# Three MLP steps in token halves at the start of an attention and MLP kernel

## What is computed

```python
x = x + layernorm(attn(layernorm(x)))          # x: (8, 512, 128)
x = x + layernorm(ffn(layernorm(x)))

def attn(x):      # linear attention, 4 heads of 32
    xn = (x - mean) / sqrt(var + eps) * gamma + beta
    q, k, v = split(xn @ w_qkv)
    k = softmax(k, over the tokens)
    context = k.T @ v; out = (q * 32 ** -0.5) @ context   # by head
    return out @ w_out + b_out + x

def ffn(x):       # 8 experts, all applied and summed
    return sum(silu(x @ Wg[e]) * (x @ Wu[e]) @ Wd[e] for e in range(8))   # 128 -> 512 -> 128
```

## Time and profile before

| | |
|---|---|
| median of 3 runs | 592.08 us (592.05 to 592.37) |
| the profiled execution, whole | 592.38 us |
| its span, first to last instruction | 590.6 us |
| TensorE busy | 583.5 us, 99% |
| VectorE, ScalarE, GpSimd busy | 444.1, 349.3, 170.5 us |
| mean granted clock of TensorE | 0.999 |

### The profile page before, as it was taken

How to read it: one execution, slowest core, us unless ns; L and a number is a source line. 1 busy time by engine, 2 the same in 40 slices (tenths; PEclk the granted TensorE clock), 3 DMA queues, 4 the chain that set the end, 5 groups by cost and what they waited for, 6 DMA issues and landing times.

```text
span 590.6 us, 9218 instructions
## 1 busy us (share of the span) xinstructions
PE 583.5 (99%) x2633; PEld 463.3 (78%) x2633; DVE 444.1 (75%) x982; ACT 349.3 (59%) x626; POOL 170.5 (29%) x205
## 2 busy tenths in 40 slices
PE   9999999999999999999999999999999999999996
PEld 5677888788887888778888788878888788888885
DVE  5996886788767886779766887678876787668666
ACT  5778666555674555745557556654567545555554
POOL 4898680037000370015500353004600032001001
PEclk9999999999999999999999999999999999999999
DMA  5522110201101020100202002020110201010000
GB/s 164 152 82 89 36 36 1 73 19 42 49 36 37 19 67 25 59 30 1 89 0 72 18 19 71 1 72 19 37 37 0 73 19 36 1 37 18 2 0 19
DMA packets 28032, 24.46 MB, mean 41 GB/s; under 512 B 3024, under 2 KB 20944, under 8 KB 27984
## 3 DMA queue, kind: packets, MB, share of 16 engines
q1 hardware_dynamic: 27408, 23.73, 12.5%
q10 hardware_dynamic: 576, 0.20, 0.1%
HBM read 15.27 MB, written 8.65 MB: 41 GB/s over the span
## 4 chain that ended last, share of the span: by engine, by line
PE 96%; DVE 1%; ACT 1%; issue 1%; POOL 0%; POOLq 0%; DVEq 0%; ACTq 0%
PE gate_ps L1010 10%; PE gate_ps L1013 10%; PE gate_ps L1011 10%; PE up_ps L1010 10%; PE up_ps L1013 10%; PE acc_ps L1010 10%; PE acc_ps L1013 10%; PE up_ps L1011 10%; PE acc_ps L1011 10%; PE att_ps L1095 1%; PE att_ps L1106 1%; PE up_ps L1154 1%; PE att_ps L1068 0%; PE att_ps L1102 0%; PE att_ps L1011 0%
## 5 line engine op out<-in xcount | busy, mean ns | idle before, releaser
L604 ACT ACTIVATE gs<-gate_ps 128x512 f32<-128x512 f32 x255 | 152.6, 598 | 210.5 <-PE gate_ps L1013 209.2
L820 DVE TENSOR_TENSOR h<-gs,up_ps 128x512 f32<-128x512 f32 x255 | 174.4, 684 | 124.5 <-PE up_ps L1013 112.9
L807 DVE TENSOR_TENSOR h_lo<-h,h_hi 128x512 fp32r<-128x512 f32 x255 | 189.7, 744 | 0.8 <-ACT h_hi L581 0.7
L581 ACT ACTIVATE h_hi<-h 128x512 fp32r<-128x512 f32 x255 | 159.3, 625 | 11.8 <-DVE h L820 10.3
L1010 PE MATMUL gate_ps<-x1nT_hi,wg_hi 128*128 128x512 f32 (+1 forms) x256 | 104.3, 407 | 0.0
L1010 PE MATMUL up_ps<-x1nT_hi,wu_hi 128*128 128x512 f32 (+1 forms) x256 | 101.1, 395 | 0.0
L1013 PE MATMUL up_ps<-x1nT_lo,wu_hi 128*128 128x512 f32 (+1 forms) x256 | 101.0, 394 | 0.0
L1013 PE MATMUL gate_ps<-x1nT_lo,wg_hi 128*128 128x512 f32 (+1 forms) x256 | 100.9, 394 | 0.0
L1011 PE MATMUL gate_ps<-x1nT_hi,wg_lo 128*128 128x512 f32 (+1 forms) x256 | 100.7, 393 | 0.0
L1011 PE MATMUL up_ps<-x1nT_hi,wu_lo 128*128 128x512 f32 (+1 forms) x256 | 100.7, 393 | 0.0
L1010 PE MATMUL acc_ps<-h_hi,wd_hi 128*128 128x512 f32 x254 | 100.6, 396 | 0.0
(11 more groups left out here) (238 smaller groups left out, 504.0 us busy)
## 6 DMA issues: line engine op xcount, KB each, us to landing
w_raw<-in_L_ffn_Wg_dram SPq DMA_DIRECT2D x8, 256.0 KB, 2.9
w_raw<-in_L_ffn_Wu_dram SPq DMA_DIRECT2D x8, 256.0 KB, 2.8
w_raw<-in_L_ffn_Wd_dram SPq DMA_DIRECT2D x8, 256.0 KB, 3.2
x_in<-in_L_attn_x_dram SPq DMA_DIRECT2D x7, 256.0 KB, 2.7
t_dram_acc<-t_blk_acc SPq DMA_DIRECT2D x7, 256.0 KB, 2.3
t_out_acc<-t_dram_acc SPq DMA_DIRECT2D x28, 64.0 KB, 2.0
out_dram<-res SPq DMA_DIRECT2D x7, 256.0 KB, 2.0
t_dram_x<-t_blk_x SPq DMA_DIRECT2D x6, 256.0 KB, 2.1
```

Of the source, the lines that this page charges most:

```text
L581: act.activation(h_hi[s % NH][:, :], h[s % NGU][:, :], ACT.Copy).then_inc(s_hhi, 1)
L604: act.activation(gs[q][:, :], gate_ps[q][:, :], ACT.Silu).then_inc(s_silu, 1)
L807: dve.tensor_tensor(h_lo[s % NH][:, :], h[s % NGU][:, :], h_hi[s % NH][:, :].bitcast(F32), ALU.subtract).then_inc(s_hlo, 1)
L820: dve.tensor_tensor(h[q][:, :], gs[q][:, :], up_ps[q][:, :], ALU.mult).then_inc(s_h, 1)
```

## The change

The start is rewritten from z to the third MLP step; the loops and tables are as they were.

- x1 of batch 0 is written by VectorE straight to SBUF (`x1[0]`), and the four copies and all waits on them go. The second half's transposes go to acc_ps instead of up_ps2.
- VectorE finishes the first half's variance and mean of z ahead of the second half's statistics, and the first half's variance of x1 ahead of the second half's x1. Likewise the first half's aggregate of x stands ahead of the wait for x's second half.
- y of the last tile is made on VectorE instead of ScalarE. `residual(0)` and `residual(1)` stand behind the A products.
- GpSimd does `split_lo(1)` ahead of z's powers, and its splits from 2 on wait for the last `first_x1n`. ScalarE's `split_hi` instructions are placed otherwise.
- The 20 fillers become 4 warm ones, 10 products with expert 0's gate weights on both sides, in five orders of reading the moving operand (two each), and 4 warm ones; 2 more stand behind the first transposes.
- Steps 0, 1 and 2 (`EARLY`) of batch 0 are taken together in halves: high products of the first half of all three steps, then the second half's transposes, low products of the first half, high ones of the second, low ones of the second.

The core of the diff:

```diff
-BUSY = {"start": 8, "w": 5, "attn": 20}
+BUSY = {"start": 8, "w": 5, "attn": 4, "end": 4, "x1n": 2}
+EARLY = 3
...
             split_lo(pool, 0)
+            split_lo(pool, 1)
             half_power("z", 0)
             half_power("z", 1)
-            split_lo(pool, 1)
             half_power("x1", 0)
             half_power("x1", 1)
+
+            pool.wait_ge(s_f_x1n, J)
             for m in range(2, 3 * FIRST):
                 split_lo(pool, m)
...
-                dve.scalar_tensor_tensor(out=tile_banks[j][:, D:2 * D], in0=tile_banks[j][:, 0:D],
+                dve.scalar_tensor_tensor(out=x1[0][:, j, :], in0=tile_banks[j][:, 0:D],
...
             first_x1_stats(0)
             first_x1_stats(1)
+            first_aggregate("x1", 0)
+            first_variance("x1", 0)
             first_x1(2)
-            first_aggregate("x1", 0)
             first_x1(3)
-            first_variance("x1", 0)
+            first_x1n(0)
+            first_x1n(1)
             first_x1_stats(2)
...
-            for j in range(J):
-                dve.wait_ge(s_f_x1ps, j + 1)
-                dve.tensor_copy(x1[0][:, j, :], tile_banks[j][:, D:2 * D]).then_inc(s_f_x1, 1)
...
-                    gate_up(t, b, s, par, first)
+                    if not first or s >= EARLY:
+                        gate_up(t, b, s, par, first)
...
+            w0, w1 = w_hi[0][:, 0, :], w_hi[0][:, 0, 0:P]
+            forms = [w0, w0.rearrange("p (a b) -> p b a", a=2), w0.rearrange("p (c a r) -> p a c r", a=2, r=16),
+                     w0.rearrange("p (c a r) -> p a c r", a=2, r=4), w0.rearrange("p (a r) -> p r a", r=32)]
+            for moving in forms:
+                for _ in range(2):
+                    pe.matmul(up_ps[0][:, :], w1, moving, start=True, stop=True)
+            keep_busy(BUSY["end"])
...
+            def early(half, which):
+
+                for s in range(EARLY):
+                    cols = slice(s * P, s * P + P)
+                    for k, ps, done in ((0, gate_ps[s], s_gate), (1, up_ps[s], s_up)):
+                        if which == "high":
+                            pe.matmul(ps[:, half], w_hi[k][:, 0, cols], x1nT_hi[0][:, half], start=True, stop=False)
+                            pe.matmul(ps[:, half], w_lo[k][:, 0, cols], x1nT_hi[0][:, half], start=False, stop=False)
+                        else:
+                            last = pe.matmul(ps[:, half], w_hi[k][:, 0, cols], x1nT_lo[0][:, half], start=False, stop=True)
+                            if half is REST:
+                                last.then_inc(done, 1)
...
+            first_n(0)
+            keep_busy(BUSY["x1n"])
...
+            pe.wait_ge(s_f_hi, 1)
+            early(HALF, "high")
+            first_n(1)
+            pe.wait_ge(s_f_lo, 1)
+            early(HALF, "low")
+            pe.wait_ge(s_x1nT_hi, 1)
+            early(REST, "high")
+            pe.wait_ge(s_x1nT_lo, 1)
+            early(REST, "low")
```

More of the change, by code:

```diff
@@ L262, in build @@
         s_f_y = sem("s_f_y")
+        s_f_y_dve = sem("s_f_y_dve")
         s_f_yb = sem("s_f_yb")
@@ L660, in _ @@
                                    bias=nm["z"][:, j:j + 1], scale=1.0).then_inc(s_f_zc, 1)
-            for m in range(3, 3 * FIRST):
-                split_hi(m)
             act.wait_ge(s_mask, 3)
             act.activation(silu_warm[:, :], zcol[:, :], ACT.Silu)
+            split_hi(3)
             act.wait_ge(s_f_n, 1)
             act.activation(x1nT_hi[0][:, HALF], att_ps[:, HALF], ACT.Copy).then_inc(s_f_hi, 1)
+            split_hi(4)
+            split_hi(5)
             act.wait_ge(s_f_n, 2)
-            act.activation(x1nT_hi[0][:, REST], up_ps[2][:, HALF], ACT.Copy).then_inc(s_x1nT_hi, 1)
+            act.activation(x1nT_hi[0][:, REST], acc_ps[:, HALF], ACT.Copy).then_inc(s_x1nT_hi, 1)
             bodies(act, body)
@@ L899, in _ @@
             dve.tensor_reduce(kmax_neg[:, 0:1], att_ps[:, :], AX_X, ALU.max, negate=True).then_inc(s_f_kmax, 1)
+            dve.wait_ge(s_f_nmr, 1)
+            dve.tensor_scalar(y[:, J - 1, :], x_in[0][:, J - 1, :], rstd["x"][:, 0, J - 1:J], nmr[:, J - 1:J], ALU.mult,
+                              ALU.add).then_inc(s_f_y_dve, 1)
             dve.wait_ge(s_f_T, 1)
@@ L919, in z_mean @@
                 dve.tensor_scalar(nm["z"][:, toks], mv["z"][:, toks, 0], -1.0, None, ALU.mult).then_inc(s_f_nm, 1)
[L921 to L931, removed]
+            for i in range(2):
+                for j in range(i * JH, i * JH + JH):
+                    dve.wait_ge(s_f_z, j + 1)
+                    first_stats("z", j, tile_banks[j][:, 0:D])
+                first_aggregate("z", i)
+                first_variance("z", i)
+                z_mean(i)
             def first_x1(j):
@@ L1023, in gate_up @@
                     pe.wait_ge(s_wlo, 3 * e + 2)
-                if first and s == 0:
-                    kinds = [(w_hi[k][:, e, cols], w_lo[k][:, e, cols], ps[q], done)
-                             for k, ps, done in ((0, gate_ps, s_gate), (1, up_ps, s_up))]
-                    for half, hi_made, lo_made in ((HALF, s_f_hi, s_f_lo), (REST, s_x1nT_hi, s_x1nT_lo)):
-                        pe.wait_ge(hi_made, 1)
-                        for hi, lo, ps, _ in kinds:
-                            pe.matmul(ps[:, half], hi, x1nT_hi[par][:, half], start=True, stop=False)
-                            pe.matmul(ps[:, half], lo, x1nT_hi[par][:, half], start=False, stop=False)
-                        pe.wait_ge(lo_made, 1)
-                        for hi, _, ps, done in kinds:
-                            last = pe.matmul(ps[:, half], hi, x1nT_lo[par][:, half], start=False, stop=True)
-                            if half is REST:
-                                last.then_inc(done, 1)
-                    return
                 for k, ps, s_done, s_free in ((0, gate_ps[q], s_gate, s_silu), (1, up_ps[q], s_up, s_h)):
@@ L1052, in down @@
                     pe.wait_ge(s_wlo, 3 * e + 3)
-                if first and s == 0:
-                    pe.wait_ge(s_f_x1, J)
                 pe.wait_ge(s_hhi, t + 1)
@@ L1233, in _, with first_n @@
             keep_busy(BUSY["attn"])
-            for j in range(J):
-                pe.wait_ge(s_f_x1n, j + 1)
-                last = pe.transpose((att_ps, up_ps[2])[j // JH][:, j % JH * P:j % JH * P + P], x1n[:, j, :], ident[:, :])
-                if j % JH == JH - 1:
-                    last.then_inc(s_f_n, 1)
+            pe.wait_ge(s_whi, 1)
+            w0, w1 = w_hi[0][:, 0, :], w_hi[0][:, 0, 0:P]
[5 more added lines that the diff above has]
+            keep_busy(BUSY["end"])
+            def first_n(i):
+                for j in tiles(i):
+                    pe.wait_ge(s_f_x1n, j + 1)
+                    last = pe.transpose((att_ps, acc_ps)[i][:, j % JH * P:j % JH * P + P], x1n[:, j, :], ident[:, :])
+                last.then_inc(s_f_n, 1)
+            def early(half, which):
[11 more added lines that the diff above has]
+            keep_busy(BUSY["x1n"])
+            pe.wait_ge(s_whi, 2)
+            pe.wait_ge(s_wlo, 2)
+            pe.wait_ge(s_f_hi, 1)
[7 more added lines that the diff above has]
+            early(REST, "low")
             bodies(pe, body)
```

36 lines of the change are left out of this document (16 added, 20 removed).

## The result

The changed kernel takes 593.5 us (median of 18 runs, 593.24 to 594.14), the kernel before 592.37 (18 runs, 591.99 to 592.78) on the same chips. The ratio is 1.002, with 95% interval 1.0013 to 1.0027: slower by about 1.1 us, as forecast (593.6 from a base of 592.08, 1.5 us slower). The interval crosses the 0.2% at which the prediction drew its line between "the same" and "slower", so that line is not decided. The profiled execution took 593.83, its span 592.0 us, 1.4 more than before.

The account below looks back on a forecast made before the run. TensorE bounds the kernel, VectorE's chain behind gate of step 0 its filling. Third down 1.5 us later: 592.38 + 1.5 = 593.9, less 0.3 for the median, 593.6 us; range 592.0 to 594.9.

Parts of the forecast that it names:

- What bounds: Whole kernel: TensorE busy 99%, its steady loop unchanged, so only its time through the first few MLP steps counts.
- A and the identity product: Start: the identity product of y moves behind A, which starts earlier; at most 0.19 us, taken as 0.15.
- z and x1: Start: reordered statistics give variance of z at 14.94, variance of x1 about 17.2, x1n(0) at 18.16 instead of 19.02.
- Fillers: TensorE ahead of the transposes: weight fillers at 0.2333 us each, all fillers 4.1 us, ending at 18.7 and just meeting x1n.
- the other end: Rival at the fillers: strided ones dear, TensorE late by 0.8 to 1.6 us, total 594.2 to 595; chance 0.20.
- One of my signs of being wrong: Fillers on TensorE: strided ones above 0.24 us between starts would show the forecast wrong.
- First product: First MLP product on TensorE: at 19.7 instead of 20.72, a gain of 1.0 us.
- Gate of step 0: First three steps in halves: gate complete with the instruction at 23.75, 1.7 us later than 22.02, shifting ScalarE and VectorE.
- The halt and the locks: First down's third product waits 1.4 us or more for h_lo; VectorE waits on GpSimd's splits; third down at 32.8, +1.5.
- The rival in which cheap locks give back most of it: VectorE's wk_lo and h_lo meet GpSimd idle or at a split's end: +0.1 to +0.8 us, 592.6; chance 0.13.
- the rival of the start alone: Start counts, pipeline filling does not: TensorE's own 0.6 us gain stands, 591.5; chance 0.15.
- The clock case: TensorE's clock falls to its lower level from 14 to 20 us; each us at half pace costs half; 0.03.

Follow-up runs that it names:

- e9: Changed kernel with eight instead of two weight fillers of each of the five reading orders; 601.4 us (one run).
- e5: Changed kernel with all ten weight fillers in the contiguous order; 593.75 us, ratio 1.0021 to the kernel before.
- e4: Changed kernel with each step's low products following its high ones in the second half; 592.49 us, ratio 1.0001 to the kernel before.
- e3: Kernel before with x1 written straight to SBUF, without the four copies and TensorE's waits on them; 594.96 us, ratio 1.0042.
- e2: Kernel before with x1 to SBUF, second transposes in acc_ps and three steps in halves; start, fillers and GpSimd's order as before; 596.64 us, ratio 1.006.
- e7: Changed kernel with GpSimd's seventh split waiting until h_lo of step 1 is made; 593.88 us, ratio 1.0027 to the kernel before.
- e12: e2 with seven warm products of 512 columns on TensorE ahead of the first down's third product; 595.12 us.

## Why the prediction was right, and where it was not

**What bounds.** Right. TensorE's loop did not change, and the whole difference was made by 33 us.

**A and the identity product.** I took 0.15 us from A starting earlier. x landed 0.11 later in this trace. With that taken out A's first product was 0.11 earlier, but A's result was not: its copy to SBUF starts at 12.53 for 12.43, 0.01 earlier. Behind it the two identity products now stand ahead of the products through the heads (12.97 for 12.78), and the first z product is 0.07 later. The step had no gain, and I had not asked who stands behind the moved instruction.

**z and x1.** The variance of z was issued at 15.27, not 14.94; the variance of x1 at 17.55, not 17.2; x1n at 18.53, not 18.16. The order did what I said: the first 0.33 is the start of z (0.15 not gained, 0.07 lost, 0.11 of landing), and the steps behind it were right to 0.04. The gain is 0.5 instead of 0.86.

**Fillers.** I took the contiguous price and called 0.43 for four of ten the other end. The truth is between: the ten hold TensorE for about 2.7 us instead of 2.33, since only the two of the last order cost 0.43. They end at 19.4 and do hold the transposes back, by 0.3. The rule that the prediction cited from the Trainium skill (SBUF — State Buffer, Door 1: The DMA port swizzle) would have made the second order dear too; e9 shows that it is not. One of my signs of being wrong, strided fillers above 0.24 between starts, did come, for two of the ten; e5 shows that it cost nothing in the time.

**First product.** 20.36 for a forecast 19.7: the gain of 1.0 was 0.36. With x1n(0) at 18.53 for 18.2 and step 3 at 25.23 for 24.5 to 24.7, these are three steps that were to show it right and did not come.

**Gate of step 0.** The count of 30 half products, transposes and wait was right to 0.1 us (3.90 for 4.03), so with the late start it was complete 2.2 later, not 1.7. e4 confirms that this is the cause.

**The halt and the locks.** The halt ahead of the first `down`'s third product was forecast at 1.4 or more and was 1.0 by the gap, 0.8 beyond the loop's pace. h_lo was done at 28.30, inside the forecast 28.0 to 28.4; but TensorE would have come to it at 27.58 and not at 26.5, since it waited for Silu, h and h_hi of step 0 itself (step 3 at 25.23, forecast 24.65, and about 0.4 more up to the first `down`). wk_lo, h_lo of step 0 and of step 1 waited about 0.5 each; I had 0.65, 0.6 and 0.7, and 1.1, 0.6 and 0.6 in the kernel before. One reading was wrong: h_lo of step 0 in the kernel before ends at 25.47 + 1.19 = 26.66, 0.54 after the split at 26.12 and not with it; it waits for the split and then does its work. Third `down` at 32.90, forecast 32.8. This was partly luck. Gate was 0.5 later than forecast; the waits came to 0.6 less than before where I had 0.35 less; and my own terms, 1.74 less 0.35, add up to 1.4 and not to the 1.5 that I wrote. e5 shows a further reason why a small error at the start does not show: what reaches the third `down` is a number of whole splits, so 0.28 at Silu of step 0 vanished there. The rival in which cheap locks give back most of it (0.13) did not come; the rival of the start alone (0.15) would have needed gate of step 0 two us earlier.

**What the prediction passed over.** It read GpSimd's wait for the last x1n only as a delay of the splits, and gave no price to x1 in SBUF without it. e3 shows that the move to SBUF costs 2.5 us if the splits are not held back, some 1.5 of them by the clock. The clock case was put at 0.03; the changed kernel did keep its clock, but e2, whose halt was 2.0 us, lost 1.5 us to it.

## What to carry to other kernels

When work is brought forward in slices over several steps, ask when the first step is complete and how long the engines behind it take, not only when the busiest engine is free again: here 0.36 us gained at the first product was paid with 2.2 us on the first finished gate. Where VectorE and GpSimd both work from SBUF, lay their instructions side by side; the long ones on GpSimd rounded the waits up here, so that a small gain ahead of them vanished (e5) and moving them moved the collision (e7). A move from PSUM to SBUF changes who may block whom, even where it saves instructions.

## What the runs showed of the hardware

- VectorE's 128x128 tensor_scalar from SBUF to SBUF beside GpSimd's 128x512 tensor_tensor: 2.50 us for two instead of 0.60 (e3); one that reads PSUM took 0.41 beside it (the kernel before). A tensor_tensor of 128x512 from SBUF: 1.18 instead of 0.68 (the changed kernel, e7). A tensor_scalar on 128x4 elements: 1.33 instead of 0.17 (e7).
- A halt of TensorE of 2.0 us behind a start with small gaps was followed by a granted clock of 0.55 and 0.60 in the next two stretches of 2 us (e2); one of 1.0 us was not (the changed kernel), and with seven products put into the 2.0 us it stayed at 1.00 too (e12). In e3 it was 0.58 behind a stretch of 2 us in which TensorE was busy for 0.33.
- A weight product of 512 columns took 0.43 from start to start when each moving element lay 32 elements behind the last, and 0.22 to 0.24 in pieces of 4 or 16, contiguous, or alternating between two places 256 elements apart (e9).
